# A fused convolution and FP4 feed-forward layer on one core: a new order of the last steps, and repeated matmuls in the tail

## The reference, cut to what matters

```python
def fp4_quant_dequant(x):                       # blocks of 16 along the last dimension
    scale = jnp.maximum(jnp.max(jnp.abs(xb), axis=-1, keepdims=True) / 6.0, 1e-12)
    xn = xb / scale
    idx = jnp.searchsorted(_MID, jnp.abs(xn))
    q = _GRID[idx] * jnp.sign(xn) * scale
...
xn = _layernorm(x)
s = _L0_attn_ref(xn, ...)                       # irfft(rfft(k) * rfft(xn)) + xn * D
gate, y = fp4_linear(xn, w_gate), fp4_linear(xn, w_up)
h = _silu(gate) * y
g = _silu(fp4_linear(h, w_down))
out = x + s * g
```

## Time and profile before

| | |
|---|---|
| median of three runs | 582.33 us (580.74 to 582.70) |
| the profiled execution | 582.21 us |
| its span, first to last instruction | 580.4 us |
| mean granted TensorE clock | 0.965 |
| PE busy | 476.4 us (82%) |
| DVE busy | 539.3 us (93%) |
| ACT busy | 409.5 us (71%) |
| POOL busy | 203.9 us (35%) |

### The profile page before, as it was taken

How to read it: one execution, slowest core, us unless ns; L and a number is a source line. 1 busy time by engine, 2 the same in 40 slices (tenths; PEclk the granted TensorE clock), 3 DMA queues, 4 the chain that set the end, 5 groups by cost and what they waited for, 6 DMA issues and landing times.

```text
span 580.4 us, 13234 instructions
## 1 busy us (share of the span) xinstructions
PE 476.4 (82%) x4956; PEld 332.1 (57%) x4956; DVE 539.3 (93%) x681; ACT 409.5 (71%) x576; POOL 203.9 (35%) x304
## 2 busy tenths in 40 slices
PE   0000376679999999999999999999999999998975
PEld 0000343235555567777777777777777777775654
DVE  6999998899999999999999999999999999998883
ACT  6945897898888877676666667676767676764543
POOL 1493001754545551111111111333333333147860
PEclk9999857889999999999999999999999999999988
DMA  6990012242222345353535353435353535339978
GB/s 174 349 286 0 2 36 92 92 99 93 90 91 92 110 128 154 100 153 102 147 101 150 102 148 104 149 96 156 99 158 95 161 96 159 96 62 155 171 103 129
DMA packets 101186, 70.80 MB, mean 122 GB/s; under 512 B 8848, under 2 KB 100752, under 8 KB 101008
## 3 DMA queue, kind: packets, MB, share of 16 engines
q1 hardware_dynamic: 93072, 61.94, 36.4%
q0 software_dynamic: 8064, 8.13, 9.6%
HBM read 61.28 MB, written 16.91 MB: 135 GB/s over the span
## 4 chain that ended last, share of the span: by engine, by line
PE 58%; DVE 25%; issue 7%; POOL 4%; ACT 3%; DMA 0%; SPq 0%; DVEq 0%; POOLq 0%
PE ps L1236 28%; PE ps L1254 10%; PE ps L1256 5%; PE ps L1245 5%; PE ps L1269 4%; PE ps L1273 4%; DVE wgu L978 4%; DVE sm L831 2%; DVE work L889 2%; POOL gbuf L522 2%; PE ps L1224 2%; DVE work L884 2%; DVE work L915 2%; DVE xh L956 1%; DVE work L850 1%
## 5 line engine op out<-in xcount | busy, mean ns | idle before, releaser
L1236 PE MATMUL ps<-wgu,work 128*128 128x512 f16 (+1 forms) x1152 | 245.0, 368 | 16.1 <-DVE work L915 14.9
L1236 PEld LDWEIGHTS ps<-wgu,work 128*128 128x128 f16 x1152 | 110.5, 99 | 128.6 <-issue 19.1
L629 ACT ACTIVATE work<-ps,con 128x704 f32<-128x704 f32 x64 | 54.2, 848 | 96.6 <-PE ps L1236 96.6
L1254 PE MATMUL ps<-wdh,work 128*128 128x256 f16 x704 | 88.5, 275 | 5.5 <-ACT gbuf L633 4.7
L624 ACT COPY work<-ps 128x1408 f16<-128x1408 f16 x64 | 84.8, 1327 | 2.2 <-PE ps L1245 1.9
L1254 PEld LDWEIGHTS ps<-wdh,work 128*128 128x128 f16 x704 | 65.8, 98 | 13.7 <-issue 5.3
L884 DVE SCALAR_TENSOR_TENSOR work<-work 128x960 f32<-128x960 bf16 (+2 forms) x67 | 72.1, 1113 | 1.6 <-ACT work L644 1.5
L522 POOL TENSOR_TENSOR gbuf<-gbuf,xh 128x256 f32<-128x256 f32 (+1 forms) x42 | 41.0, 1048 | 91.9 <-DVE work L897 77.8
L889 DVE SCALAR_TENSOR_TENSOR work<-work 128x1920 f16<-128x1920 bf16 (+3 forms) x36 | 69.7, 1936 | 1.2
L850 DVE TENSOR_TENSOR work<-work,ps 128x960 f32<-128x960 f32 (+2 forms) x63 | 68.4, 1126 | 1.1
L831 DVE TENSOR_REDUCE sm<-work 128x120 f32<-128x1920 f32 (+2 forms) x32 | 66.4, 2074 | 1.3
(11 more groups left out here) (155 smaller groups left out, 676.2 us busy)
## 6 DMA issues: line engine op xcount, KB each, us to landing
work<-kpad SPq DMA_DIRECT2D x64, 512.0 KB, 3.8
work<-L_attn_u SPq DMA_DIRECT2D x33, 256.0 KB, 3.4
gbuf<-u_rev SPq DMA_DIRECT2D x4, 2048.0 KB, 18.7
out<-gbuf POOLq DMA_DIRECT2D x7, 1024.0 KB, 10.3
out<-L_attn_u SPq DMA_DIRECT2D x1, 768.0 KB, 5.5
out<-gbuf POOLq DMA_DIRECT2D x1, 768.0 KB, 7.8
work<-L_ffn_w_down SPq DMA_DIRECT2D x1, 704.0 KB, 6.7
work<-L_ffn_w_gate SPq DMA_DIRECT2D x1, 640.0 KB, 4.5
```

The source lines that it names most:

```text
L1236: last = T.matmul(p_gu[:, a:b], xT[par][:, t, c, :], wgu[:, part, c % 2, a:b], start=(n == 0), stop=(n == len(todo) - 1))
L1254: T.matmul(dst, hT[t][:, c, :], wdh[:, c, :], start=(c == 0), stop=False)
```

## The change

On GpSimd, parts 0 and 1 of the first twelve groups of four tiles are made before step 28; which products and stores come in steps 28 to 31 is now a list (`CLOSING`), with tiles 48 to 55 among them, and a finished group of eight is stored behind the next step's tables (only the last at the end of step 31). GpSimd makes the tables of step 32 too. It stores seven times and no more. On VectorE step 32 uses these tables, waits for them (tb_p), and keeps its reciprocals in PSUM; then tiles 56 to 63 are multiplied and have u added in five pieces (`LAST`), each stored by SyncE. u of these tiles is loaded into the space of the convolution's kernels once the convolution is over, and the last sequence is no longer copied to the output ahead. On ScalarE step 32 has silu_out(59) first, h_copy(61) between the two squares, and the silu of tiles 60 and 61 behind them. On TensorE down(61) goes to a PSUM tile of its own, and `keep_running` repeats a matmul of 256 columns into an unused part of PSUM, 12 times ahead of each of the last two groups of transposes and 8 times ahead of down(62).

```diff
--- before.py
+++ after.py
@@ -107,6 +107,7 @@
         tpl_words = [carve(4 * 2 * P) for _ in range(2)]
         tpl = [words.bitcast(F16).rearrange("p (r c) -> p r c", c=2 * P) for words in tpl_words]
         LATE = used[0]
+        u_last = work[:, LATE - 2 * 4 * 2 * P:LATE].rearrange("p (t h) -> p t h", t=8)
         vb = [carve(NC * BLK) for _ in range(2)]
         rbuf = carve(NC * BLK // 2)
         xhl_xT = work[:, used[0]:used[0] + 8 * H]
@@ -115,7 +116,6 @@
         xT_words = carve(4 * H)
         xT = [xT_words[:, 2 * H * i:2 * H * (i + 1)].bitcast(F16).rearrange("p (t c k) -> p t c k", t=2, c=4) for i in range(2)]
         xin = [v[:, 2 * I:].rearrange("p (t h) -> p t h", t=2) for v in vb]
-        u_last = carve(2 * H).rearrange("p (t h) -> p t h", t=2)
         by_blk = [v.rearrange("p (c k) -> p c k", k=BLK) for v in vb]
         d_bf, r_f16 = (rbuf.bitcast(dt).rearrange("p (c k) -> p c k", k=BLK) for dt in (BF16, F16))
 
@@ -238,7 +238,6 @@
         g_a = sem("g_a")
         o_in = sem("o_in")
         f_p = sem("f_p")
-        f_l = sem("f_l")
         f_y = sem("f_y")
         f_t = sem("f_t")
         f_st = sem("f_st")
@@ -369,7 +368,12 @@
         PEEL = 4
         TURNS = (2, 3, 0, 1)
         FIRST = NT // 4 - 2
-        OPEN = [min(it for it in range(NP) if groups_before(it + 1) >= q1 * C2 // G8) for q0, q1 in PARTS]
+        OPEN = (19, 24)
+        LAST = ((NT - 8, NT - 6), (NT - 6, NT - 4), (NT - 4, NT - 2), (NT - 2, NT - 1), (NT - 1, NT))
+        CLOSING = {S_TAIL: ((12, 0), (12, 1), (0, 2), (1, 2), (2, 2), (3, 2)),
+                   S_TAIL + 1: ((4, 2), (5, 2), (6, 2), (7, 2)),
+                   S_TAIL + 2: ((8, 2), (9, 2), (10, 2), (11, 2), (13, 0)),
+                   S_TAIL + 3: ((12, 2), (13, 1), (13, 2))}
 
         @block.sync
         def _(sp):
@@ -408,7 +412,6 @@
                              zero.bitcast(F16).rearrange("p (r i) -> p r i", i=P)[:, :, 0:w]).then_inc(k_pad, 16)
 
             load_x(2, 0)
-            sp.dma_start(u_last, u_t[:, NT - 2:NT, :]).then_inc(u_in, 16)
 
             def store_filter():
                 sp.wait_ge(k_split, 3)
@@ -426,8 +429,8 @@
 
             def copy_input(i):
 
-                rows = LSEQ if i < SEQS - 1 else LSEQ - 2 * P
-                sp.dma_start(out[i:i + 1, 0:rows], u[i:i + 1, 0:rows]).then_inc(o_in, 16)
+                if i < SEQS - 1:
+                    sp.dma_start(out[i:i + 1], u[i:i + 1]).then_inc(o_in, 16)
 
             for it in range(PEEL):
                 load_x(it + 3, (it + 1) % 2)
@@ -454,10 +457,12 @@
                     load_t(n, n % 2)
             for n in range(2 * groups_before(NP - 3) + 2, H // 4):
                 load_t(n, n % 2)
-            for n in range(2):
+            sp.wait_ge(cv_h, H // 4)
+            sp.dma_start(u_last, u_t[:, NT - 8:NT, :]).then_inc(u_in, 16)
+            for n, (t0, t1) in enumerate(LAST):
                 sp.wait_ge(f_t, n + 1)
-                sp.dma_start(out_t[:, NT - 2 + n:NT - 1 + n, :], gbuf[:, NT - 2 + n:NT - 1 + n, :]).then_inc(f_st, 16)
-            sp.wait_ge(f_st, 32)
+                sp.dma_start(out_t[:, t0:t1, :], gbuf[:, t0:t1, :]).then_inc(f_st, 16)
+            sp.wait_ge(f_st, 16 * len(LAST))
 
         @block.gpsimd
         def _(pool):
@@ -550,42 +555,59 @@
             pool.wait_ge(k_split, 2)
             nc.gpsimd.tensor_tensor(kl, kt, kh, ALU.subtract).then_inc(k_split, 1)
 
-            todo = [(n, part) for n in range(FIRST) for part in range(len(PARTS))]
-            made, sent = [0], [0]
-
-            def some_gated(it, room):
-
+            todo = [(n, part) for n in range(FIRST - 2) for part in range(2)]
+            made, sent, stores = [0], [0], []
+
+            def some_gated(it):
+
+                room = 4
                 ready = [(n, part) for n, part in todo if 4 * n + 3 <= it * 2 - 5 and it >= OPEN[part]]
-                for n, part in sorted(ready, key=(lambda job: (job[1], job[0])) if it < OPEN[2] else None):
+                for n, part in sorted(ready, key=lambda job: (job[1], job[0])):
                     room -= 2 if part == 0 else 1
                     if room < 0:
                         break
                     gated(n, part)
                     todo.remove((n, part))
                     made[0] += 1
-                    if all(m // 2 != n // 2 for m, _ in todo):
-                        room -= 3
-                        sent[0] += 1
-                        pool.wait_ge(f_p, made[0])
-                        add_out(n // 2 * 8, 4 * n + 4)
-
-            for it in range(NP):
+
+            def closing_gated(it):
+
+                assert not todo
+                for n, part in CLOSING[it]:
+                    gated(n, part)
+                    made[0] += 1
+                    if part == 2 and n % 2:
+                        stores.append(n // 2 * 8)
+
+            def some_stores():
+
+                if stores:
+                    pool.wait_ge(f_p, made[0])
+                    if sent[0] == 0:
+                        pool.wait_ge(o_in, 16 * (SEQS - 1))
+                for t0 in stores:
+                    add_out(t0, t0 + 8)
+                    sent[0] += 1
+                stores.clear()
+
+            for it in range(NP + 1):
                 tables(it, it < NP - 2, it >= 1)
+                some_stores()
                 if it < NP - 2:
                     pool.wait_ge(x_hl, 2 * (it + 3))
-                else:
+                elif it < NP:
                     pool.wait_ge(hl_v, it)
                 if it < S_CONV:
                     a_low(it * 2)
                     a_low(it * 2 + 1)
-                if it == OPEN[2]:
-                    pool.wait_ge(o_in, 16 * SEQS)
-                if it >= OPEN[0]:
-                    some_gated(it, 4 if it < OPEN[2] else 8)
-            some_gated(NP, NP)
-            pool.wait_ge(f_l, 1)
-            add_out(4 * FIRST, NT - 2)
-            pool.wait_ge(f_out, 16 * (sent[0] + 1))
+                if OPEN[0] <= it < S_TAIL:
+                    some_gated(it)
+                elif S_TAIL <= it < NP:
+                    closing_gated(it)
+                    if it == NP - 1:
+                        some_stores()
+            assert sent[0] == FIRST // 2
+            pool.wait_ge(f_out, 16 * sent[0])
 
         @block.scalar
         def _(act):
@@ -794,8 +816,14 @@
                 step(it, it % 2, True, True, it < NP - 3, True, True, True, cv=groups_of(it), c0=groups_before(it))
             step(NP - 2, 0, False, True, False, True, True, True)
             step(NP - 1, 1, False, False, False, True, True, True)
-            step(NP, 0, False, False, False, False, True, True)
-            silu_out(NT - 3, 1, 0)
+            h_copy(NT - 4, 0)
+            silu_out(NT - 5, 1, 1)
+            square(NP, 1, False, True, 0)
+            h_copy(NT - 3, 1)
+            square(NP, 1, False, True, 1)
+            silu_out(NT - 4, 0, 0)
+            silu_out(NT - 3, 1, 0, p_dn2)
+            down_scale(NP - 1, 1)
             for t in range(2):
                 h_copy(NT - 2 + t, t, (p_hT, p_hT2)[t])
             for t in range(2):
@@ -848,22 +876,6 @@
                     v = by_blk[pp][:, c]
                     sc = rs[:, c].rearrange("p (c k) -> p c k", k=1).to_broadcast([P, c.stop - c.start, BLK])
                     V.tensor_tensor(v, v, sc, ALU.mult).then_inc(v_v, 1)
-
-            def h_largest(it):
-
-                own.settle()
-                after(dve, gs_a, it - 1)
-                own.mark(V.tensor_reduce(mt, s_[:, HB].rearrange("p (t b) -> p t b", t=2), AX_X, ALU.max))
-                own.settle()
-                V.tensor_scalar(p2.bitcast(U32), mt.bitcast(U32), EXPONENT, None, ALU.bitwise_and).then_inc(p2_v, 1)
-
-            def h_normalise(it):
-
-                dve.wait_ge(p2_v, it)
-                own.mark(V.reciprocal(ti, p2))
-                own.settle()
-                sh = s_[:, HB].rearrange("p (t b) -> p t b", t=2)
-                return V.tensor_tensor(sh, sh, ti.rearrange("p (t o) -> p t o", o=1).to_broadcast([P, 2, NB]), ALU.mult)
 
             def twice(cols):
 
@@ -1137,31 +1149,32 @@
             step(NP - 2, 0, False, True, True)
             step(NP - 1, 1, False, True, True)
 
-            scales(NP, 1, False, True)
-            inverse(1, False, True)
-            h_largest(NP)
-            own.mark(h_normalise(NP))
-            scale_hi(HB)
-            scale_lo(HB)
+            def gate_y(t0, t1):
+
+                dve.wait_ge(g_a, t1)
+                gc = by_two(gbuf[:, t0:t1, :])
+                return V.tensor_tensor(gc, gc, yv[:, :, t0:t1, :].rearrange("p q t c -> p t q c"), ALU.mult)
+
+            def finish(n):
+
+                t0, t1 = LAST[n]
+                gate_y(t0, t1).then_inc(f_y, 1)
+                dve.wait_ge(f_y, n + 1)
+                V.tensor_tensor(gbuf[:, t0:t1, :], gbuf[:, t0:t1, :], u_last[:, t0 - (NT - 8):t1 - (NT - 8), :], ALU.add
+                                ).then_inc(f_t, 1)
```

(36 more changed lines are left out.)

8 lines of the change are left out of this document (4 added, 4 removed).

## The result

The changed kernel took 572.67 us (median of four runs, 572.47 to 573.40), the kernel before beside it 581.54 us (four runs, 580.58 to 582.70): a ratio of 0.9851, 95% interval 0.9827 to 0.9874, 1.5% faster. The sign was forecast and so was most of the mechanism, but the time lies 1.2 us under the low end of the range (573.9): the tail behind the last sum, forecast at 4.0 us, took 2.16. The profiled execution took 572.49 us with a span of 570.7, so 1.79 us lie outside it.

A forecast was written before the change was run, and what follows sets the result against it. Behind 514 us it took VectorE's waits for GpSimd's tables, a full TensorE and the last step as bounds. Last sum 570.0, end 4.0 and 1.81 outside the span gave 575.8 us; forecast 574.8 to 576.8, range 573.9 to 579.6.

The forecast's parts named there:

- the end: From VectorE's last sum to the end of the span: 4.0 us, bounds 3.4 and 4.9, before 4.27.
- What bounds it: Behind 514 us: VectorE waiting for GpSimd's tables, then a full TensorE in steps 30 and 31, then the last step.
- The terms 1.95, 0.15 and 1.2: Gains in us from removing VectorE's waits for GpSimd's tables in steps 29, 30 and 31; h_mult(63) 3.3 us earlier.
- Step 32 on VectorE: Six small scale operations go and two scalings get faster, one small reduction comes in: net 2.4 us.
- Step 32 on ScalarE and TensorE: Earlier silu_out(59) and a separate PSUM tile: down(60) starts at 555.8, down(61) at 558.15, gaps 0.5 us at most.
- The repeats: 32 extra TensorE matmuls at 0.109 us each, ahead of real work: cost 1.7 us and give nothing if the clock stays up.
- no gap over 0.6 us is left: TensorE's idle gaps in the tail, as laid out; the argument against a fall of the granted clock there.
- The fourth: Shorter end: last 128 KB land about 1 us sooner, and step 29 gains its bound of 2.14; 574.2 us, chance 0.10.
- The first: GpSimd's tables of step 32 come late, starting at 556.3: 577 to 577.6 us, chance 0.12.
- The third: The stores become the bound, seven starting 8 us later than before: 578.2 us, chance 0.06.
- The fifth: Slower: the granted clock falls in the tail before down(61) and stays down: 586 to 587 us, chance 0.04.

The follow-up runs named there:

- stores_ahead: The changed kernel with GpSimd's stores issued ahead of the next tables, as in the kernel before, in steps 28 to 30: 577.29 us.
- own_scales: The changed kernel with step 32's scales made by VectorE as before and no GpSimd tables for that step: 573.12 us.
- old_scalar_order: The changed kernel with ScalarE's old order in step 32 and down(61) back in its old PSUM tile, all repeats kept: 576.74 us.
- before_end: The kernel before with only the new end (five VectorE pieces stored by SyncE, no 768 KB GpSimd store): 578.23 us against 580.52, ratio 0.9959.
- no_repeats: The changed kernel without the 32 repeated matmuls: 573.40 us, against 573.29 for the changed kernel beside it.

## Why the prediction was wrong, point by point

Up to the last sum the forecast was right: 570.0 us with a mark of 134.76, a distance of 435.24, and 435.35 was measured. The step that failed is the term behind it, the end: 4.0 us were taken, 2.16 measured. The rest of the miss is the profiled execution on which the sum was built.

**What bounds it, and steps 29 to 31: right.** The terms 1.95, 0.15 and 1.2 gave h_mult(63) 3.3 us sooner; it came 3.24 sooner (416.65 us from the mark for 419.89): 1.97 up to gate_up(60), 0.14 from there to gate_up(62), 1.13 from there to h_mult(63). stores_ahead gives 1.97, 0.14 and 1.40 back, and shows that a wait beside a full TensorE is worth 0.14 us of 1.22. In step 29 I had the tables run into the roundings; the last table product ended at 519.07, 0.17 us into the first of them (518.90), since the products took 0.71 us each and the tables began 0.9 us sooner than I had them. The rule of the Trainium skill (SBUF — State Buffer, Who interferes with whom) had therefore little to act on there. The trace agrees with it in the next operation, which began at 519.04 beside the rounding and took 1.13 us instead of 0.22, and in the rounding of step 32, held to 1.21.

**Step 32 on VectorE: the mechanism right, the term too large.** 2.4 us were forecast, 1.84 measured (7.89 for 9.73). Missing were the 0.32 by which the last table product holds the first rounding and a wait of 0.24 for the square. And 1.19 of the 1.84 don't need the tables: own_scales has them with GpSimd quiet, as its two scalings then take 1.69 us.

**Step 32 on ScalarE and TensorE: right, with some luck.** down(60) and down(61) started within 0.3 us of the forecast (554.47 and 556.65, with 1.57 added 556.04 and 558.22, for 555.8 and 558.15), and old_scalar_order gives the order a value of 2.6 us. VectorE's second half of h ended 0.6 us later than forecast (561.42, with 1.57 added 562.99, for 562.4). It cost nothing only because T(63) stood behind the second twelve repeats anyway; from there to the last sum it was 7.12 us, where the forecast had 7.6.

**The repeats: wrong on what they give.** I had the order without them 1.7 us faster, "as long as the clock stays up by itself". It mostly doesn't: three of three profiles show it fall within T(63), and of the five other runs without repeats only one has a span that speaks for a clock that stayed up. The price was right to 0.01 us a repeat. What failed here is the step that no gap over 0.6 us is left: I worked that out with the repeats in place and carried it over to the order without them, where 1.91 us of gap open. With the repeats as placed the balance is plus 0.55 us against these profiles, and about minus 1.1 against that one run (span 569.6, the shortest of the changed kernel 570.7); with twelve in the gap alone it is plus 1.7 (435.90 less 433.86, without the 0.35 of the moved store).

**The end: the term that was mis-sized.** I took 4.0 us from the last sum to the end of the span, from 4.27 and a landing of 3.7; it is 2.16. The 4.27 had GpSimd's 768 KB store in them, which I named and priced at 0.3 us. before_end, with that store gone and the last sum where it was (441.31 us from the mark for 441.37), has a tail of 2.11, 2.16 us less. This alone is 1.84 of the 3.1 us by which the forecast was too high. The page DMA: Bandwidth & Descriptors of the Trainium skill (the two cost components) has 2.0 us fixed, fitted on DMAs that GpSimd issues, and by it I noted a tail of 2.8. The 128 KB stores, which SyncE issues, land after medians of 1.7 us in before_end and 2.0 in after, so the trace agrees with the page and not with the row that I preferred, and the time by it, 574.6, would have been nearer.

**What was not in the sum.** 1.57 us lie between the two profiles in the first 135 us. I built on one profiled execution, 582.21 us, which had a late mark; after's four runs lie at 572.5 to 573.4 and the later ones of the same kernel at medians of 573.29 and 573.77. So 575.8 less 1.84 for the tail is 574.0. The 1.57 less of the profile of after, the 0.11 by which the last sum came late, and the 0.18 by which after's median lies above its profiled execution (572.49) lead from there to 572.67. The range had no room for the 1.57. That part of the miss is chance: against the later medians it would have been 2.0 to 2.5 us in all.

**The rivals.** None came about as written. The fourth (shorter end) had the right side and too small a size, and its number doesn't follow from its terms: 1 us and 0.19 off 575.8 leave 574.6, not 574.2. The first did not: the tables of step 32 started at 553.42, with 1.57 added 554.99, as the forecast had them and not at 556.3. The third (stores as the bound) did not either: the stores began 4.5 us later than in before (520.12, with 1.57 added 521.69, for 517.21) and not 8, and the last one, issued at 552.45, landed after 11.8 us, 4.3 us ahead of the end of the last sum. The fifth was real in its mechanism, but it took the repeats' removal to bring it about.

## What to carry to other kernels

A landing time read beside another transfer isn't the price of the store: take the shortest landing of a store of that size that stands alone, and ask which transfer ends the span once the compute in front of it is faster. A wait of one engine is worth only what the engine that is full there also waits. Repeated matmuls belong into the gap and not ahead of ready work; there each costs its full time (0.108 us here), and the gap has to be looked for in the order without them.

## What was not expected of the hardware

The clock fell 0.3 to 0.5 us behind a gap of 1.91 us with eleven transposes on either side of it (no_repeats, three profiles), and stayed at 1.00 through one of 2.17 us with transposes ahead of it and matmuls behind (old_scalar_order, one profile). The length of the idle time alone doesn't tell it, the spans speak for a difference from one execution to the next, and what decides was not settled. An accumulating store holds GpSimd's next operation back by 1.0 us, two in a row by 1.9 to 2.1 us (stores_ahead), though their rows last 3.2 to 3.3. And the operation right behind a store is itself longer: 0.87 us instead of 0.22 at 553.42, while the store's row runs to 554.01 and VectorE's operations have PSUM on one side, so not all of the 1.10 us of the earlier trace rows need be VectorE's doing. The first 135 us of the same program differ by up to 1.8 us from one execution to the next.
